# First attention's score core: maxima products ahead of the value products in each unit

## The chip, the cores and the metric

The kernel runs on one core of a Trainium2 chip. The metric is the device time of one execution in microseconds; lower is better. Three executions of the kernel before took 3728.84, 3730.03 and 3730.82 us, so its median is 3730.03 us.

## The reference

The whole program is four gated blocks of cross attention and feed-forward on a residual stream `x` of shape (4, 512, 512). The change is in the first attention only, which is this part of it:

```python
def _ln(t, w, b):
    m = jnp.mean(t, axis=-1, keepdims=True)
    v = jnp.var(t, axis=-1, keepdims=True)
    return (t - m) * jax.lax.rsqrt(v + EPS) * w + b
def _attn(q, k, v):
    s = jnp.einsum('bhqd,bhkd->bhqk', q, k) * SCALE
    p = jax.nn.softmax(s, axis=-1)
    return jnp.einsum('bhqk,bhkd->bhqd', p, v)
y_dca, y_main = y[:, -DCA:, :], y[:, :-DCA, :]          # DCA = 16 of the 512 context rows
q = _ln((x @ Wq + bq).reshape(b, s1, H, HD), qn_w, qn_b)  # H = 16 heads, HD = 32
ctx = _attn(qT, k, v)            # over the 496 main context rows
ctx_dca = _attn(qT, k_dca, v_dca)  # over the 16 others
ctx = ctx + DCA_WEIGHT * ctx_dca
return ctx @ Wo + bo
x = x + jnp.tanh(g_xattn[0]) * _L0_xattn_ref(_layernorm(x), ctx_1024, ...)
```

The later layers (a sign-weight feed-forward, a second attention, an int8 feed-forward, a state-space scan, two expert layers and a fourth attention with 32 heads) are not touched.

## The kernel before

Every layer is a run of blocks, and in a block each engine has its own program, in the order in which it is written; the programs meet at semaphores. The first attention has a weights block, a projection block, a core block and an output block. The change is in `attention_core_block` (L1640), in the branch for the first attention (`rope` false). The last attention calls the same function with `rope` true and takes the other branch.

**How the core is tiled.** There are 4 batches of 16 heads. A group is 2 heads of a batch (TG = 32 groups), and a unit is one of the 4 tiles of 128 context rows for the 2 heads of a group (TU = 128 units, UPG = 4 to a group). What a unit n needs of TensorE:

- `scores_t(n)` (L1841): two products of 128x512 into `ac_S`, the transposed scores. ScalarE takes their exponential into `ac_PT` (L1941).
- `values(n)` (L1857): the value products of the exponentials into `ac_o`, in float32. In the last unit of a group four more records follow, into `ac_t` (L1863), for the 16 other context rows.
- The softmax needs each query's maximum, and needs it before the scores. So separate maxima products (`scores(m)`, L1812) are made well ahead: 256 in all, 8 to a group (4 query tiles x 2 heads), the first 18 before any unit and then 2 to a unit through `more(n)` (L1879) until none is left, which is in the units 0 to 118. VectorE reduces each with two instructions (L1960 over 496 columns, L1962 over 16) into `ac_nmax`, and signals `max_done` (printed as maxima_81).
- Once the 8 maxima of a group are there, VectorE scales them into `ac_mx` (L1973), TensorE transposes them (`maxima_rows(g)`, L1829, in the first unit of a group, from `at_rows`), ScalarE copies the transposed rows to `ac_mrow` (L1932, signal `rows_ev`), and SyncE's queue sends them into a row of `QT` by four small DMAs (L1729). The scores of that later group then come out with the maximum subtracted.
- When a group is done, ScalarE copies `ac_o` and `ac_t` into `ac_oT` (L1923, L1925), TensorE transposes those in the next group's second and third unit (`group_transposes`, L1876), and VectorE divides by the sums and adds (L1984 to L1991, signal `a_done`). After each batch, the result is stored by a DMA of 1 MB (L1734), behind the row DMAs on the same queue, and VectorE's first division of the next batch waits for that.

**What sets the order.** TensorE's order is that of the loop below. ScalarE's is written too: in the first unit of a group it does the exponential, then the two copies L1923 and L1925 of the group before, which wait for the last value product; in the second unit the exponential, and behind it the copy of the rows, L1932.

**The ring.** `psM` has two slots. The maxima products and the transposed rows share them in turn, in the order in which the list `use` names them. A user may write only when the user two places before it has been read. The order in `use` is: two maxima, then, in a group's first unit, the rows.

```python
                for n in range(TU):
                    if n + 1 < TU:
                        scores_t(n + 1)
                    if n:
                        values(n - 1)
                    more(n)
                    if n in at_rows:
                        maxima_rows(at_rows[n])
```

Of the kernel before, what the change touches and what calls it, by code (L numbers as in the profile page):

```python
# [1639 lines left out]
def attention_core_block(nc, env, w, rope):  # L1640
# [20 lines left out]
    with ExitStack() as ctx:  # L1661
# [32 lines left out]
        def of_unit(n):  # L1694
            g, u = divmod(n, UPG)
            return g, u // NP, u % NP
# [19 lines left out]
        def chunk(g, i):  # L1716
            h = g % NG * GH + i
            return (h // 2, 64 * (h % 2), 64) if rope else (h, 0, P)
# [78 lines left out]
        def _(pe):  # L1797
# [6 lines left out]
            def scores(m):  # L1804
                g, j, i = of_maximum(m)
                b = g // NG
                if m % (NG * NMG) == 0 and b:
                    pe.wait_ge(kq_in[b % 2], 32 * ((b + 1) // 2 if b % 2 else b // 2))
                slot, previous = ring["max", m]
                reader_of(previous)  # L1810
                c, base, n = chunk(g, i)
                nc.tensor.matmul(psM[:, slot, :], QT[b % 2][base:base + n, j, c, :], KT[b % 2][base:base + n, :, c, :],  # L1812
                                 start=True, stop=True).then_inc(s_done, 1)

            def maxima_rows(g):
                pe.wait_ge(m_ready, g + 1)
                if rope:
                    if g >= 3:
                        pe.wait_ge(a_done, g - 2)
                    if g:  # L1820
                        pe.wait_ge(rows_ev, g)
                    bank = pd[:]
                else:
                    slot, previous = ring["rows", g]
                    reader_of(previous)
                    bank = psM[:, slot, :]
                out = bank.bitcast(F16)
                for j in range(TPB):
                    last = nc.tensor.transpose(out[0:NR, j * P:(j + 1) * P], mx[:, g % 2, j, :], env.id16[:])  # L1829
                last.then_inc(rows_T, 1)  # L1830

            def scores_t(n):
                g, kt, p = of_unit(n)
                b = g // NG
                if n % UPG == 0:
                    pe.wait_ge(row_in[g % 2], 16 * NR * (g // 2 + 1))
                if n >= 2:
                    pe.wait_ge(exp_done, n - 1)
                for i in range(2):
                    c, base, k = chunk(g, 2 * p + i)  # L1840
                    last = nc.tensor.matmul(psS[:, 2 * (n % 2) + i, :], KT[b % 2][base:base + k, kt, c, :],  # L1841
                                            QT[b % 2][base:base + k, :, c, :], start=True, stop=True)
                last.then_inc(sT_done, 1)

            def values(n):

                g, kt, _ = of_unit(n)
                b = g // NG
                if n + 1 - NP == b * UB:
                    pe.wait_ge(v_ready, b + 1)  # L1850
                if kt == 0 and g:
                    pe.wait_ge(o_ev, g)
                pe.wait_ge(exp_done, n + 1)
                for m in range(n + 1 - NP, n + 1):
                    for i in range(2):
                        r = 2 * of_unit(m)[2] + i
                        last = nc.tensor.matmul(po[r * VC:(r + 1) * VC, :], V[b % 2][:, kt, g % NG * GH + r, :],  # L1857
                                                PT[:, m % PTB, i, :], start=(kt == 0), stop=(kt == TPB - 1))
                if not rope and kt == TPB - 1:
                    if g:  # L1860
                        pe.wait_ge(a_done, g * NOUT)
                    for i in range(2):
                        last = nc.tensor.matmul(pd[i * VC:(i + 1) * VC, :], Vd[b % 2][:, g % NG * GH + i, :],  # L1863
                                                PT[:, n % PTB, i, :], start=True, stop=True)
                last.then_inc(pv_done, NP)

            def group_transposes(g, i):
                pe.wait_ge(o_ev if rope else oT_done, g + 1)
                if rope:
                    if g:  # L1870
                        pe.wait_ge(a_done, g)
                    pe.wait_ge(rows_ev, min(TG, g + 3))
                elif i:
                    pe.wait_ge(a_done, g * NOUT + i)
                for j in range(TPB):
                    last = nc.tensor.transpose(psT[:, j, :], oT[:, i, j * P:(j + 1) * P], env.id32[:])  # L1876
                last.then_inc(ot_T, 1)

            def more(n):  # L1879
                for m in range(AHEAD + 2 * n, min(TM, AHEAD + 2 * n + 2)):  # L1880
                    scores(m)
# [5 lines left out]
            if rope:  # L1887
                scores_t(1)
                for n in range(0, TU, 2):
                    if n + 2 < TU:  # L1890
                        scores_t(n + 2)
                    more(n)
                    values(n + 1)
                    more(n + 1)
                    if n + 3 < TU:
                        scores_t(n + 3)
                    for k in (n, n + 1):
                        if k in at_rows:
                            maxima_rows(at_rows[k])
                    if n % UPG == 2 and n > UPG:  # L1900
                        group_transposes(n // UPG - 1, 0)
            else:
                for n in range(TU):
                    if n + 1 < TU:
                        scores_t(n + 1)
                    if n:
                        values(n - 1)
                    more(n)
                    if n in at_rows:
                        maxima_rows(at_rows[n])  # L1910
                    if n >= UPG and n % UPG in (1, 2):
                        group_transposes(n // UPG - 1, n % UPG - 1)
                values(TU - 1)
# [964 lines left out]
```

## Time and profile before

| | |
|---|---|
| median of 3 executions | 3730.03 us (3728.84 to 3730.82) |
| profiled execution, its own time | 3727.34 us |
| its span | 3725.6 us |
| TensorE busy | 2626.4 us, 70% |
| VectorE busy | 2344.9 us, 63% |
| ScalarE busy | 1584.9 us, 43% |
| GpSimd busy | 997.7 us, 27% |

The core block of the first attention runs from 229 us to 622 us of this span, some 10% of it. The busy shares above are means over stages that have different limits, so they tell little of this block; it has to be read by its own stretches, and for a change of order by the timeline of one group, instruction by instruction. In a timeline row the time is the start, the next number the time from the first start to the last end, and in brackets is how long the engine had sat idle and what ended that. PEld is TensorE's loading of weights, which runs beside its products.

### The profile page before, as it was taken

The numbers are of one execution on the slowest core, as the hardware profiler recorded it, in microseconds if no ns is written. First come the engines' busy times: TensorE is split into PE (matmuls) and PEld (weight loads), VectorE is DVE, ScalarE is ACT, GpSimd is POOL, SyncE is SP. The second block draws the span as 40 slices with busy tenths as digits, with TensorE's granted clock in tenths as the row PEclk, the third lists the DMA queues.
The fourth block names the chain that finished last, engine by engine and source line by source line (L and its number), as shares of the span: only waits on it lengthen the run. The fifth ranks groups of instructions, "written<-read, shape, count | busy, mean of one in ns | idle before, by whom it ended". The sixth has DMA issues, their size and how long they took to land. (4 is left out here: it accounts for less than half of the span.)

```text
span 3725.6 us, 45742 instructions
## 1 busy us (share of the span) xinstructions
PE 2626.4 (70%) x13916; PEld 1206.9 (32%) x13916; DVE 2344.9 (63%) x4155; ACT 1584.9 (43%) x2191; POOL 997.7 (27%) x874
## 2 busy tenths in 40 slices
PE   3978888699665365275576559981978897748991
PEld 1532223344322122021121247760522222324660
DVE  6655664555735634598898766655668886455663
ACT  3544443144221034344444235551646766122870
POOL 5760000000000211376676322215640000001434
PEclk9979999799776587598898779995979999869995
DMA  3541101010000000000000157753531100112994
GB/s 128 204 153 71 57 12 57 15 46 34 0 3 9 19 0 0 0 1 0 0 0 0 46 182 239 237 173 113 219 140 69 46 12 24 65 49 79 321 304 153
DMA packets 148635, 305.98 MB, mean 82 GB/s; under 512 B 18323, under 2 KB 65439, under 8 KB 146038
## 3 DMA queue, kind: packets, MB, share of 16 engines
q1 hardware_dynamic: 125542, 223.49, 17.0%
q0 software_dynamic: 22928, 80.49, 6.8%
q8 instruction: 79, 1.29, 0.1%
q14 instruction: 86, 0.70, 0.1%
HBM read 210.34 MB, written 93.32 MB: 82 GB/s over the span
## 5 line engine op out<-in xcount | busy, mean ns | idle before, releaser
L1960 DVE TENSOR_REDUCE ac_nmax<-ac_M 128x1 f32<-128x512 f32 (+1 forms) x768 | 495.5, 680 | 197.8 <-PE ac_M L1812 196.0
L1941 ACT ACTIVATE ac_PT<-ac_S 128x1024 f32<-128x1024 f32 x384 | 380.5, 1018 | 220.4 <-PE ac_S L1841 220.4
L2680 PE MATMUL sc_y<-sc_hc,ident 128*128 128x512 f32 x512 | 294.0, 658 | 141.0 <-POOL sc_hc L2656 140.5
L2656 POOL TENSOR_TENSOR sc_hc<-sc_h,sc_cs 128x512 f32<-128x512 f32 x256 | 324.3, 1268 | 174.5 <-DVE sc_h L2758 170.6
L2758 DVE TENSOR_TENSOR_SCAN sc_h<-sc_dA,sc_dB 128x512 f32<-128x512 f32 x256 | 309.9, 1212 | 9.7 <-ACT sc_dA L2718 9.7
L1857 PE MATMUL ac_o<-ac_PT,ac_V 128*32 128x512 f32 (+1 forms) x1536 | 281.4, 621 | 7.4 <-ACT ac_PT L1941 7.0
L2718 ACT ACTIVATE sc_dA<-sc_dl,sc_A 128x512 f32<-128x512 f32 x256 | 176.4, 690 | 177.3 <-DVE sc_h L2758 177.3
L2680 PEld LDWEIGHTS sc_y<-sc_hc,ident 128*128 128x128 f32 x512 | 79.5, 193 | 333.6 <-POOL sc_hc L2656 330.5
L2750 DVE TENSOR_TENSOR sc_dB<-ss_du,sc_b 128x512 f32<-128x512 f32 x256 | 168.4, 659 | 15.8 <-PE sc_b L2670 15.8
L955 DVE SCALAR_TENSOR_TENSOR mo_up16l<-mo_up,mo_up16h 128x1408 f16<-128x1408 f32 (+1 forms) x80 | 117.1, 1465 | 72.8 <-ACT mo_up16h L899 72.1
L802 POOL DMA_INDIRECT mo_g<-normalised,mo_cur x112 | 145.8, 1302 | 61.3 <-POOL mo_cur L798 44.2
L2332 POOL TENSOR_TENSOR f_o<-f_o,f_bias 128x512 f16<-128x512 f32 x16 | 20.7, 1291 | 523.4 <-DVE f_o L2381 523.4
L1812 PE MATMUL ac_M<-KT,QT 64*128 64x512 f16 (+1 forms) x384 | 135.6, 425 | 32.7 <-DVE ac_nmax L1960 19.5
L855 PE MATMUL mo_pu<-mo_y16h,mo_up16h 128*128 128x256 f16 (+1 forms) x832 | 127.1, 276 | 27.5 <-DVE mo_up16l L955 12.6
L224 PE MATMUL ln_yt<-ident,ln_y 128*128 128x128 f32 x256 | 68.7, 433 | 103.1 <-DVE ln_y L200 103.1
L593 PE MATMUL ex_po<-ex_dn,ex_midh 128*128 128x512 f16 x384 | 137.6, 383 | 5.3 <-DVE ex_acc L657 5.3
L647 DVE SCALAR_TENSOR_TENSOR ex_midl<-ex_mid,ex_midh 128x512 f16<-128x512 f32 x80 | 55.2, 692 | 127.9 <-ACT ex_midh L540 127.9
L1812 PE MATMUL ac_M<-ac_KT,ac_QT 64*128 64x512 f16 (+1 forms) x384 | 120.4, 389 | 20.9 <-DVE ac_nmax L1960 18.5
L962 DVE SCALAR_TENSOR_TENSOR mo_dn16l<-mo_dn,mo_dn16h 128x1024 f16<-128x1024 f32 x80 | 83.0, 1062 | 71.2 <-ACT mo_dn16h L906 68.5
L1376 PE MATMUL ap_t<-ident,ap_y 128*128 128x128 f32 x128 | 20.4, 284 | 151.5 <-DVE ap_y L1562 151.5
L855 PE MATMUL mo_pu<-mo_y16l,mo_up16h 128*128 128x256 f16 (+1 forms) x832 | 125.8, 274 | 0.0
L855 PE MATMUL mo_pu<-mo_y16h,mo_up16l 128*128 128x256 f16 (+1 forms) x832 | 125.3, 273 | 0.0
(480 smaller groups left out, 5879.8 us busy)
## 6 DMA issues: line engine op xcount, KB each, us to landing
slot_results<-mo_o SPq DMA_DIRECT2D x56, 512.0 KB, 3.9
mo_up<-in_w_gate SPq DMA_DIRECT2D x24, 704.0 KB, 5.4
mo_up<-in_w_up SPq DMA_DIRECT2D x24, 704.0 KB, 7.1
keys_t<-ap_kto SPq DMA_DIRECT2D x32, 512.0 KB, 2.6
queries_t<-ap_qto SPq DMA_DIRECT2D x32, 512.0 KB, 2.7
mo_up<-in_exp_up SPq DMA_DIRECT2D x32, 512.0 KB
mo_dn<-in_exp_down SPq DMA_DIRECT2D x32, 512.0 KB
mo_dn<-in_w_down SPq DMA_DIRECT2D x24, 512.0 KB
```

The lines of the kernel that those rows point to most:

```text
L593: last = nc.tensor.matmul(po[j][:], (mid_h, mid_l)[a][0:n, tb % 2, c, j * P:(j + 1) * P], dn16[w][h][0:n, c, :], start=(i == 0), stop=(i = ...
L802: pool.indirect_dma_start(g[:, w, h, :], None, rows, bass.IndirectOffsetOnAxis(cur[:, w, h:h + 1], 0)).then_inc(g_in[w], 16)
L855: last = nc.tensor.matmul(pu[q][0:n, j, :], up16[h][:, w, j, k, c * P:c * P + n], y16[a][:, w, k, :], start=(i == 0), stop=(i == len(passe ...
L1812: nc.tensor.matmul(psM[:, slot, :], QT[b % 2][base:base + n, j, c, :], KT[b % 2][base:base + n, :, c, :], start=True, stop=True).then_inc( ...
L1857: last = nc.tensor.matmul(po[r * VC:(r + 1) * VC, :], V[b % 2][:, kt, g % NG * GH + r, :], PT[:, m % PTB, i, :], start=(kt == 0), stop=(kt ...
L1941: nc.scalar.activation(PT[:, n % PTB, :, :], psS[:, 2 * (n % 2):2 * (n % 2) + 2, :], ACT.Exp, scale=SCALE / (SQK * SQK)).then_inc(exp_done, 1)
L1960: last = v.tensor_reduce(out[:, :, 0], sc[:, 0:MAIN], AX.X, ALU.max)
L2656: nc.gpsimd.tensor_tensor(hc[:, m % RC, :], h[:, m % RH, :], cs[:, n % 2, :], ALU.mult).then_inc(hc_done, 1)
L2680: nc.tensor.matmul(py[:, c, :], env.id32[:], hc[:, m % RC, :], start=(n == 0), stop=(n == NS - 1)).then_inc(y_mm, 1)
L2718: nc.scalar.activation(dA[:, m % RA, :], dl[:, c, :], ACT.Exp, scale=A[:, c, n:n + 1]).then_inc(dA_done, 1)
L2750: nc.vector.tensor_tensor(dB[:, m % RB, :], at(du, b * KD + c), pb[:], ALU.mult).then_inc(dB_done, 1)
L2758: nc.vector.tensor_tensor_scan(h[:, m % RH, :], dA[:, m % RA, :], dB[:, m % RB, :], 0.0, ALU.mult, ALU.add).then_inc(h_done, 1)
```

## The change

In each unit the call `more(n)` (two maxima products) now stands ahead of `values(n - 1)` and not behind it. The list `use`, which gives the slots, is unchanged, and so are all other engines' programs.

```diff
@@ -1903,9 +1903,9 @@
                 for n in range(TU):
                     if n + 1 < TU:
                         scores_t(n + 1)
+                    more(n)
                     if n:
                         values(n - 1)
-                    more(n)
                     if n in at_rows:
                         maxima_rows(at_rows[n])
```

First place, TensorE where one group ends and the next begins (`ac_t<-ac_PT,ac_Vd` are the last value products of a group, `ac_M<-ident,ac_mx` the transposed rows; maxima_81 is the count of reduced maxima, rows_ev_84 the count of rows that ScalarE has copied, group_ev_88 ScalarE's copy of `ac_o`). Before:

```order
L1863 MATMUL ac_t<-ac_PT,ac_Vd 64x512 [waits attn_norm_91]
L1863 MATMUL ac_t<-ac_PT,ac_Vd 64x512
L1812 MATMUL ac_M<-KT_1,QT_1 128x512 [waits maxima_81] x2
L1829 MATMUL ac_M<-ident,ac_mx 4x128 [waits maxima_81,max_rows_82]
L1829 MATMUL ac_M<-ident,ac_mx 4x128 x3
L1841 MATMUL ac_S<-QT_1,KT_1 128x512 [waits exp_86]
L1841 MATMUL ac_S<-QT_1,KT_1 128x512
L1857 MATMUL ac_o<-ac_PT,ac_V 64x512 [waits exp_86,group_ev_88]
L1857 MATMUL ac_o<-ac_PT,ac_V 64x512
L1812 MATMUL ac_M<-KT_1,QT_1 128x512 [waits maxima_81]
L1812 MATMUL ac_M<-KT_1,QT_1 128x512 [waits rows_ev_84]
L1876 MATMUL ac_t<-ident,ac_oT 128x128 [waits group_copied_89]
```

The same place now:

```order
L1812 MATMUL ac_M<-KT_1,QT_1 128x512 [waits maxima_81] x2
L1857 MATMUL ac_o<-ac_PT,ac_V 64x512 [waits exp_86]
L1857 MATMUL ac_o<-ac_PT,ac_V 64x512
L1863 MATMUL ac_t<-ac_PT,ac_Vd 64x512 [waits attn_norm_91]
L1863 MATMUL ac_t<-ac_PT,ac_Vd 64x512
L1829 MATMUL ac_M<-ident,ac_mx 4x128 [waits maxima_81,max_rows_82]
L1829 MATMUL ac_M<-ident,ac_mx 4x128 x3
L1841 MATMUL ac_S<-QT_1,KT_1 128x512 [waits exp_86]
L1841 MATMUL ac_S<-QT_1,KT_1 128x512
L1812 MATMUL ac_M<-KT_1,QT_1 128x512 [waits maxima_81]
L1812 MATMUL ac_M<-KT_1,QT_1 128x512 [waits rows_ev_84]
L1857 MATMUL ac_o<-ac_PT,ac_V 64x512 [waits exp_86,group_ev_88]
```

The maxima products of the group's first unit moved from behind the `ac_t` products to ahead of the whole value step, and the transposed rows now follow the value products directly. Those of the second unit, the second of which waits for ScalarE's copy of the rows, moved from behind the value products of that unit to ahead of them.

Second place, TensorE in the third and fourth unit of a group, from its second transpose of results on (attn_norm_91 is `a_done`, row_in0_77 the landing of the row DMAs). Before:

```order
L1876 MATMUL ac_t<-ident,ac_oT 128x128 [waits attn_norm_91,group_copied_89]
L1876 MATMUL ac_t<-ident,ac_oT 128x128 x3
L1841 MATMUL ac_S<-QT_1,KT_1 128x512 [waits exp_86,row_in0_77]
L1841 MATMUL ac_S<-QT_1,KT_1 128x512
L1857 MATMUL ac_o<-ac_PT,ac_V 64x512 [waits exp_86]
L1857 MATMUL ac_o<-ac_PT,ac_V 64x512
L1812 MATMUL ac_M<-KT_1,QT_1 128x512 [waits maxima_81] x2
L1841 MATMUL ac_S<-QT_1,KT_1 128x512 [waits exp_86]
```

And now:

```order
L1876 MATMUL ac_t<-ident,ac_oT 128x128 [waits attn_norm_91,group_copied_89]
L1876 MATMUL ac_t<-ident,ac_oT 128x128 x3
L1841 MATMUL ac_S<-QT_1,KT_1 128x512 [waits exp_86,row_in0_77]
L1841 MATMUL ac_S<-QT_1,KT_1 128x512
L1812 MATMUL ac_M<-KT_1,QT_1 128x512 [waits maxima_81] x2
L1857 MATMUL ac_o<-ac_PT,ac_V 64x512 [waits exp_86]
L1857 MATMUL ac_o<-ac_PT,ac_V 64x512
L1841 MATMUL ac_S<-QT_1,KT_1 128x512 [waits exp_86]
```

Here the pair of maxima moved ahead of the value products too. The orders of VectorE, ScalarE, GpSimd and SyncE are the same before and now.

## Rows read from the trace of the kernel before

**Rows 1.** Stretches; columns: us, busy us of PE, PEld, DVE, ACT, POOL (instructions), PEclk, DMA share, GB/s

```profile
273.89:338.90 65.01, 60.82 (x288) 20.34 (x288) 43.87 (x133) 32.20 (x43) 7.54 (x8) 1.00 0.09 33
440.00:450.00 10.00, 8.24 (x40) 2.70 (x36) 5.83 (x18) 3.07 (x4) 0.23 (x1) 1.00 0.45 179
460.00:468.00 8.00, 7.81 (x23) 2.38 (x24) 3.86 (x13) 1.02 (x1) 0.00 (x0) 0.60 0.00 0
```

**Rows 2.** Waits, 244 to 622 us: who waited for whom, us, times, longest

```profile
PE ac_M L1829 <- DVE ac_nmax L1962: 21.5, 30, 0.7
PE ac_t L1876 <- DVE ac_A L1986: 10.9, 3, 3.6
```

**Rows 3.** Timeline of PE, one full group, 500 to 512 us

```profile
500.50 0.60 PE L1812 MATMUL ac_M<-KT,QT 128*128 128x512 f16 x2
501.83 0.38 PE L1829 MATMUL ac_M<-ident,ac_mx 128*4 128x128 f16 x4 [0.72 <-DVE ac_nmax L1962]
502.14 0.61 PE L1841 MATMUL ac_S<-QT,KT 128*128 128x512 f16 x2
502.68 1.08 PE L1857 MATMUL ac_o<-ac_PT,ac_V 128*64 128x512 f32 x4
503.69 0.60 PE L1812 MATMUL ac_M<-KT,QT 128*128 128x512 f16 x2
504.13 0.60 PE L1876 MATMUL ac_t<-ident,ac_oT 128*128 128x128 f32 x4
506.55 0.60 PE L1876 MATMUL ac_t<-ident,ac_oT 128*128 128x128 f32 x4
506.99 0.59 PE L1841 MATMUL ac_S<-QT,KT 128*128 128x512 f16 x2
509.49 1.08 PE L1857 MATMUL ac_o<-ac_PT,ac_V 128*64 128x512 f32 x4
510.40 1.03 PE L1863 MATMUL ac_t<-ac_PT,ac_Vd 128*64 128x512 f32 x4
511.36 0.60 PE L1812 MATMUL ac_M<-ac_KT,ac_QT 128*128 128x512 f16 x2
```

**Rows 4.** Timeline of ACT, the same group

```profile
500.61 0.60 ACT L1923 ACTIVATE ac_oT<-ac_o 128x512 f32<-128x512 f32 x1 [2.83 <-PE ac_t L1863]
501.11 0.59 ACT L1925 ACTIVATE ac_oT<-ac_t 128x512 f32<-128x512 f32 x1
501.58 1.03 ACT L1941 ACTIVATE ac_PT<-ac_S 128x1024 f32<-128x1024 f32 x1
502.49 0.57 ACT L1932 ACTIVATE ac_mrow<-ac_M 4x512 f16<-4x512 f16 x1
```

**Rows 5.** Timeline of DVE, the same group

```profile
500.93 0.68 DVE L1960 TENSOR_REDUCE ac_nmax<-ac_M 128x1 f32<-128x496 f32 x1 [1.34 <-PE ac_M L1812]
507.87 0.20 DVE L1984 RECIPROCAL ac_rec<-ac_t 128x8 f32<-128x8 f32 x1
508.95 0.67 DVE L1960 TENSOR_REDUCE ac_nmax<-ac_M 128x1 f32<-128x496 f32 x1
510.28 0.16 DVE L1962 TENSOR_REDUCE ac_nmax<-ac_M 128x1 f32<-128x16 f32 x1
```

**Rows 6.** Timeline, 238 us: PEld waiting for the copy of the rows

```profile
238.00 0.59 ACT L1932 ACTIVATE ac_mrow<-ac_M 4x512 f16<-4x512 f16 x1 [15.97 <-PE ac_M L1829]
...
238.63 0.10 PEld L1812 LDWEIGHTS ac_M<-KT,QT 128*128 128x128 f16 x1 [0.51 <-ACT ac_mrow L1932]
```

**Rows 7.** Timeline of PE where it sat idle longer

```profile
445.97 0.61 PE L1841 MATMUL ac_S<-QT,KT 128*128 128x512 f16 x2 [1.76 <-DMA QT<-ac_mrow]
460.19 1.08 PE L1876 MATMUL ac_t<-ident,ac_oT 128*128 128x128 f32 x4 [3.62 <-DVE ac_A L1986]
467.93 0.61 PE L1812 MATMUL ac_M<-KT,QT 128*128 128x512 f16 x2
609.27 0.61 PE L1841 MATMUL ac_S<-ac_QT,ac_KT 128*128 128x512 f16 x2 [1.53 <-DMA ac_QT<-ac_mrow]
```

## The prediction

> **What bounds the kernel now.** The change touches only the core block of the first attention, so I read that block alone, in four steps. First the table of stretches: in steady state TensorE is busy 60.82 of 65.01 us at a granted clock of 1.00, while VectorE has 43.87 and ScalarE 32.20 [rows 1]. TensorE is the bound there, with a gap of about 7%. Then the list of waits: 30 times TensorE waited for VectorE ahead of the transposed rows (L1829), 21.5 us in all and never more than 0.7; and 3 times, up to 3.6 us, for a division that itself waits for the store at the end of a batch [rows 2]. Then the timeline of one group, which tells what the gap is. In the first unit of a group the two maxima products start at 500.50; each takes half of 0.44 (503.69 to 504.13 is a pair). The transposed rows take the ring slot of the first of them, so they wait until that one is reduced, and start at 501.83: 501.83 - 500.50 - 0.44 = 0.89 us in which TensorE issues nothing [rows 3]. VectorE starts the reduction only 0.43 after the product starts [rows 5]. From 500.50 to the same place at 511.36 a group takes 10.86 us [rows 3]; of the 30 distances between transposed rows in the timeline 23 have this length.
>
> The last view is ScalarE's timeline beside it, since the ring has a second edge. The second maxima product behind the transposed rows takes their slot, and must wait until ScalarE has copied them (the order prints it as the wait for rows_ev). In a group's first unit ScalarE copies `ac_o` at 500.61 and `ac_t` at 501.11, when the last value product is done; then comes an exponential at 501.58, and only then the copy of the rows, from 502.49 to 503.06 [rows 4]. Before the change the product that needs it is due at 503.69 + 0.22 = 503.91 [rows 3], so that edge costs nothing, with 0.8 us to spare.
>
> **The change, term by term, for one full group.** I call 0 the moment at which TensorE has issued the last value product of a group (500.50 in the trace of before). Nothing is added or removed; 119 pairs of maxima products move ahead of 118 value steps (unit 0 has none), and on each side of a value product the neighbours change.
>
> *Removed:* the 0.89 us. The maxima of the first unit now come ahead of the value products and the `ac_t` products, 1.9 us (509.49 to 511.36 [rows 3]) earlier. Their first reduction is over before the rows are due, by over half a microsecond. The rows can start at 0.
>
> *Added:* the wait for ScalarE. It can't be moved, because its two copies are released by the last value product as before, and ScalarE's order is the same; so the copy of the rows still ends at 503.06 - 500.50 = 2.56. Where the trace shows TensorE waiting for this copy, the weights load starts at 238.63 for a copy that ends at 238.59, so 0.04 later [rows 6]: the second maximum goes at 2.60. Without the wait it would go at 0.97, that is, rows 0.31 (501.83 to 502.14), scores 0.44, first maximum 0.22. The new wait is 1.63 us. What is queued behind the waiting product: the value products, the transposes and the scores of the next units, in short all that TensorE has. No other engine relieves it. The value products of the second unit now start at 2.60 + 0.22 + 0.10 = 2.92, where the 0.10 is what the scores before a value step take beyond a pair's 0.44 (502.14 to 502.68 is 0.54). Before it was 502.68 - 500.50 = 2.18 [rows 3]. **So this part of the group gets 0.74 us longer**, the removed gap counted in.
>
> *Behind that,* from these value products to the next 0: before 8.68 us (502.68 to 511.36), now the same instructions, three pairs of maxima among them as before, so 8.68 again, if nothing new waits.
>
> *A second wait, small:* VectorE in the third and fourth unit. The second transpose of results is issued at 2.92 + 3.87 - 0.44 = 6.35 (before it, 502.68 to 506.55, stood one pair more), and ends at 6.95. VectorE's division and addition follow at about 7.00 and take 1.08 (507.87 to 508.95), then two maxima 1.49 (508.95 to 510.44) [rows 5]: 9.57. The second maximum of the next first unit needs that slot at 6.35 + 0.44 + 0.44 + 0.54 + 1.01 + 0.44 + 0.22 = 9.44 (transpose, scores, pair, values, scores, one maximum). It waits some 0.2 us. Before, this reduction had the value products in between.
>
> *A possible saving:* a value step takes 1.01 when float16 products follow (502.68 to 503.69) and 0.91 when float32 ones do (509.49 to 510.40) [rows 3]. Now the transposes of results, which are float32, follow a value step directly in two units of a group. The trace has no such pair of neighbours, so this is worth 0 to 0.2 us a group; I take half.
>
> Sum for a full group: + 0.74 + 0.2 - 0.1 = **+ 0.84 us**, with bounds of + 0.5 (no second wait, all of the saving) and + 1.1 (no saving, second wait of 0.35). Over 23 full groups that is 19.3 us.
>
> *The seven other distances* hold a stall by a DMA or are the first or the last. Three of them hold the wait for the store of a batch [rows 2]. The store is queued behind the row DMAs, which start with the copy of the rows, at the same 2.56; so TensorE is released there at the same moment as before, and both the removed gap and the new wait vanish in that stall. What remains is one pair of maxima more between release and next 0, 0.44, or twice that at the lower clock, and part of the second wait. The groups where scores wait for a late row DMA work in the same way. I take + 0.6 for six of these, 3.6, and 0 for the first (there ScalarE has no results to copy, so the gap goes and little comes). In all **+ 23 us**.
>
> The clock. After the batch stall of 3.62 us the products run slower until 467.93 [rows 7]; over 460 to 468 the granted clock is 0.60 [rows 1], that is, mostly the 1.2 GHz level. But after waits of 1.76 and 1.53 us at 445.97 and 609.27 products take the same time as before (0.61 for a pair) [rows 7], and over 440 to 450 it is 1.00 [rows 1]. The new wait, 1.63 less the tail of the product before it, is a little under these. So I price the clock at nothing.
>
> Against that stands a rule of the Trainium skill (TensorE: Matmul & The Clock Gate, A second HAM failure mode): a kernel whose TensorE idles briefly but often between groups of products can swing between the two clock levels. By it the sum would be that of the clock rival below. The trace so far disagrees, with 30 gaps of 0.7 us at 1.00.
>
> **Numbers.** The profiled execution took 3727.3 us, 2.7 below the median of 3730.0, which is within what executions differ. 3727.3 + 23 = 3750 for a profiled one, 3730 + 23 = **3753 us** for the median. About 0.2%, or 7.5 us, is what a measurement of this kernel can tell from no change.
>
> **Rivals.**
> - *Faster: the copy of the rows is not late.* If something frees the slot within a microsecond, the 0.89 goes 30 times and little comes: - 27 us, 3703. It decides at a wait of 0.89: below it the change gains. For it: the exponential ahead of the copy has its scores early, and ScalarE sat idle 2.83 us before it [rows 4]. Against: the exponential is written behind both copies, which wait for the last value product, and the order of ScalarE is unchanged; the trace shows these four back to back. 5%.
> - *No change: the two about cancel.* If float16 to float32 switches save 0.1 us in most of 119 units rather than in 60, 8 to 10 us come back, and without the second wait (4 us) the sum is + 23 - 9 - 5 = + 9, 3739; a little more puts it below 7.5. For it: the 0.10 is seen at both sides of a value step. Against: in a unit without transposes the number of switches stays. 6%.
> - *Much slower: the clock.* If each new wait brought the lower level, as the batch stall does, then the stretch from the second transpose to the next 0 takes 467.93 - 460.19 = 7.74 in place of 511.36 - 506.55 = 4.81 [rows 3, 7], 2.9 us a group, 29 times: + 85, so 3730 + 23 + 85 = 3838. 4%.
> - My forecast has the other 85%: 23 x 0.5 plus little, + 12, at one end, 23 x 1.1 and 1 us for each other group, + 32, at the other.
>
> Faster by over 0.2%: 5%. Within: 6%. Slower by over 0.2%: 89%. Forecast's own span is 3742 to 3762; for 8 in 10, with the spread of runs and the cancelling case's upper part, 3738 to 3768.
>
> **What would show it.** In the profile after: the wait of L1829 for VectorE gone; a new wait of the second maximum (L1812) for `ac_mrow` L1932, some 30 times, 1.4 to 1.6 us each; a distance between transposed rows of 11.6 to 11.9 us in place of 10.86; a few tenths of waiting for `ac_nmax` once a group; a granted clock of 1.00 in the steady stretches; ScalarE's four rows in the same spacing. The block from first scores to last should be some 23 us longer, and every later block the same. If L1812 doesn't wait for L1932, the main step is wrong; if the distance is under 10.9, so is the sign; if the clock falls in steady groups, the size is.

## The result: 23 to 30 us slower, with a new wait behind the transposed rows

| | before | after |
|---|---|---|
| median, first comparison | 3729.78 us (4 runs) | 3759.70 us (4 runs, 3758.02 to 3761.70), ratio 1.0080, 95% interval 1.0063 to 1.0098 |
| median, the change once more | 3727.82 us (19 runs) | 3750.96 us (4 runs, 3750.04 to 3760.30), ratio 1.0067, 1.0047 to 1.0087 |
| span of the profiled execution | 3725.6 us | 3759.9 us, and 3748.2 us in the second |
| core block, from its first product to the first of the output block | 405.7 us | 432.4 us, and 429.1 us |

The change costs 30 us by the first comparison and 23 us by the second. In the core block it is 26.8 us in the first profile and 23.4 in the second; the rest, in the first profile only, lies in blocks that the change does not touch (see the last section). Of the 26.8 and 23.4 us, 2.1 and 0.7 come before the first unit's transposed rows, where TensorE's order is still that of before and the first scores wait for their row DMA (3.39 us before, 5.46 and 4.14 after).

The profile after. First the table of stretches over six full groups (71.23 us, against 65.01 in [rows 1]):

```profile
273.75:344.98 71.23, 62.36 (x290) 20.68 (x288) 44.49 (x132) 32.40 (x42) 5.85 (x7) 1.00 0.08 28
```

The clock is 1.00 as before. The stretch is 6.2 us longer and TensorE's busy time 1.5 us more, so 4.7 us of the loss are plain idle time. The rest is the tails of products that now stand alone (0.38 and 0.39 where a pair shows 0.60) and slower transposes, both seen in the timeline below. The list of waits of TensorE from 262 us to the end of the block says which:

```profile
PE ac_M L1812 <- ACT ac_mrow L1932: 42.9, 29, 1.5
PE ac_t L1876 <- DVE ac_A L1986: 10.9, 4, 3.4
PE ac_S L1841 <- DMA ac_QT<-ac_mrow: 5.3, 2, 3.8
```

The waits of L1829 for VectorE, 21.5 us in [rows 2], are gone from here on. In their place stand 42.9 us, 29 times, in which the second maximum waits for ScalarE's copy of the rows. The waits for the store at batch ends are nearly what they were (3.36 us each, against 3.62 [rows 7]; the fourth in the list, 0.85 us, stands at the end of the block and stood there before too, behind the window of [rows 2]). The timeline of TensorE in one full group, to be laid beside [rows 3]:

```profile
504.65 0.39 PE L1829 MATMUL ac_M<-ident,ac_mx 128*4 128x128 f16 x4
504.97 0.60 PE L1841 MATMUL ac_S<-QT,KT 128*128 128x512 f16 x2
505.41 0.38 PE L1812 MATMUL ac_M<-KT,QT 128*128 128x512 f16 x1
507.27 0.39 PE L1812 MATMUL ac_M<-KT,QT 128*128 128x512 f16 x1 [1.48 <-ACT ac_mrow L1932]
507.59 1.08 PE L1857 MATMUL ac_o<-ac_PT,ac_V 128*64 128x512 f32 x4
508.60 0.66 PE L1876 MATMUL ac_t<-ident,ac_oT 128*128 128x128 f32 x4
509.09 0.59 PE L1841 MATMUL ac_S<-QT,KT 128*128 128x512 f16 x2
...
513.96 0.77 PE L1812 MATMUL ac_M<-KT,QT 128*128 128x512 f16 x2
514.66 1.08 PE L1857 MATMUL ac_o<-ac_PT,ac_V 128*64 128x512 f32 x4
515.57 1.03 PE L1863 MATMUL ac_t<-ac_PT,ac_Vd 128*64 128x512 f32 x4
516.52 0.39 PE L1829 MATMUL ac_M<-ident,ac_mx 128*4 128x128 f16 x4
```

And ScalarE beside it, to be laid beside [rows 4]:

```profile
504.77 0.60 ACT L1923 ACTIVATE ac_oT<-ac_o 128x512 f32<-128x512 f32 x1 [3.43 <-PE ac_t L1863]
505.26 0.59 ACT L1925 ACTIVATE ac_oT<-ac_t 128x512 f32<-128x512 f32 x1
505.74 1.03 ACT L1941 ACTIVATE ac_PT<-ac_S 128x1024 f32<-128x1024 f32 x1
506.65 0.57 ACT L1932 ACTIVATE ac_mrow<-ac_M 4x512 f16<-4x512 f16 x1
```

The moment called 0 in the prediction is 504.65. The rows go there without a gap. ScalarE's four instructions have the spacing of before to 0.02 us, the copy of the rows ends at 507.22, that is at 2.57, and the second maximum goes at 2.62. Had it been free it would have gone at 505.63, 0.22 behind the first: a wait of 1.64 us in TensorE's issue (the profile lists 1.48, since the product before it was still running). The distance from one group's transposed rows to the next is 11.87 us, against 10.86, in 23 of 30 cases.

Three small terms are visible too, one wait and two slower transposes. The pair at 513.96 takes 0.70 and not 0.53 until the value products follow, so 0.17 of waiting for VectorE. And each of the two transposes of results, now directly behind a value step, takes 0.49 (508.60 to 509.09) where it took 0.44 [rows 3].

So a full group can be written as a ledger. Without any wait and with the neighbours of before it is 10.86 - 0.89 = 9.97 us. Add 1.64 + 0.17 + 2 x 0.05: 11.88, against 11.87 measured.

### The profile page after: what moved, and what is told of

It reads as the page before. It is cut to its first block and busy times, and to the rows that moved or that the text cites. A ratio compares the mean times of both kernels' runs of the same rounds, so it can differ in the third digit from the quotient of the medians.

```text
span 3759.9 us, 45742 instructions
## 1 busy us (share of the span) xinstructions
PE 2641.8 (70%) x13916; PEld 1211.9 (32%) x13916; DVE 2349.0 (62%) x4155; ACT 1586.3 (42%) x2191; POOL 1000.4 (27%) x874
```

## The experiments

Two theories were set against each other. A: the loss is the ring's second edge, the wait for ScalarE's copy of the rows. B: it comes from the value products' new neighbours and from waits for VectorE, in all units alike. Each kernel's group length comes from the distances between the L1829 rows of its timeline, most of which agree to a few hundredths; the ratio is to the kernel before on the same chip. Each was compared with 19 to 23 runs of before.

### e1: the pair of the second unit stays behind

```diff
-                    more(n)
+                    if n % UPG in (0, 2, 3):
+                        more(n)
                     if n:
                         values(n - 1)
+                    if n % UPG not in (0, 2, 3):
+                        more(n)
```

> The change is kept in the first, third and fourth unit of a group; in the second unit the two maxima go behind the value products as before. Theory A (the loss is the wait of the second maximum in the second unit for ScalarE's copy of the rows, at 2.60 us behind the last value product of the group): that maximum is then due at 0.31 + 0.54 + 1.01 + 0.22 = 2.08, the wait falls from 1.48 to about 0.5 us and lies behind the value products; I expect a group of about 10.9 us and 3730 to 3740 us. Theory B (the loss comes from the new neighbours of the value products and from waits for VectorE in all units alike): only a quarter of the 30 us goes, 3750 us or more.

Measured: 3734.6 us median (10 runs), ratio 1.0021, 1.0010 to 1.0033; most groups 10.86 us. TensorE from one group to the next:

```profile
498.60 0.61 PE L1841 MATMUL ac_S<-QT,KT 128*128 128x512 f16 x2
...
503.42 0.39 PE L1829 MATMUL ac_M<-ident,ac_mx 128*4 128x128 f16 x4
503.73 0.60 PE L1841 MATMUL ac_S<-QT,KT 128*128 128x512 f16 x2
504.27 1.08 PE L1857 MATMUL ac_o<-ac_PT,ac_V 128*64 128x512 f32 x4
505.28 0.39 PE L1812 MATMUL ac_M<-KT,QT 128*128 128x512 f16 x1
506.03 0.39 PE L1812 MATMUL ac_M<-KT,QT 128*128 128x512 f16 x1 [0.36 <-ACT ac_mrow L1935]
```

The second maximum waits 506.03 - 505.50 = 0.53, not 1.64, though three of four pairs are still ahead: theory A. But the gap is not won back. The scores at 498.60 wait for the row DMAs, whose landing nobody had waited for in a full group of before; the weights row says so:

```profile
498.60 0.12 PEld L1841 LDWEIGHTS ac_S<-QT,KT 128*128 128x128 f16 x2 [0.38 <-DMA QT<-ac_mrow]
```

Their due time was 498.29 (0.49 behind the transposes at 497.80), so they wait 0.31. Ledger: 9.97 + 0.53 + 0.31 + 0.05 = 10.86. That a group is as long as before is a coincidence: two new waits and a slower transpose add up to the gap that was removed.

### e2: ScalarE copies the rows ahead of the exponential

```diff
-                before = n - (3 if rope else 1)
+                before = n - (3 if rope else 0)
                 if before in at_rows:
                     group_rows(at_rows[before])
```

> TensorE's order is that of the change; ScalarE copies the rows directly behind its two copies of results and ahead of the exponential of the second unit. Theory A: the copy ends 0.91 us earlier (502.49 less 501.58 in the trace of before), the wait of the second maximum falls from 1.48 to about 0.6 us, a group from 11.87 to 11.0, and the time by 29 x 0.9 = 26 us to about 3734 us. Theory B (neighbours and VectorE): no change, 3760 us.

Measured: 3728.67 us (10 runs), ratio 1.0000, 0.9990 to 1.0010; groups 10.97 us. TensorE's order is exactly that of the change:

```profile
500.40 0.38 PE L1812 MATMUL ac_M<-KT,QT 128*128 128x512 f16 x1
501.35 0.39 PE L1812 MATMUL ac_M<-KT,QT 128*128 128x512 f16 x1 [0.57 <-ACT ac_mrow L1932]
```

The wait in the issue falls from 1.64 to 501.35 - 500.62 = 0.73, by the 0.91 that the exponential took, and the group by 0.90. The ledger closes here too: 9.97 + 0.73 + 0.17 + 0.10 = 10.97. The whole loss of time went with ScalarE's order; this is what theory A asks, and theory B is out as the main cause.

### e3: only the first unit's pair ahead

The set `(0, 2, 3)` of e1 is `(0,)` here.

> Only in the first unit of a group the two maxima go ahead of the value products. This takes the 0.89 us gap ahead of the transposed rows away and leaves the second unit as it was. If that gap is a loss of its own, 23 to 27 us are gained: 3705 us. If, as a count of VectorE's steps says, the pair of the fourth unit (still behind its value products) and this pair now lie only a pair and the scores apart (0.44 + 0.44 us, against 2 x 0.67 us of reductions), TensorE waits for VectorE there instead: some 0.9 us, and the rows copy is waited for by 0.5 us more: then no gain but a loss, 3740 to 3750 us.

Measured: 3755.89 us (4 runs), ratio 1.0072, 1.0055 to 1.0089; groups 11.76 us. The sign is that of the second guess, the size is above it.

```profile
503.56 0.60 PE L1841 MATMUL ac_S<-QT,KT 128*128 128x512 f16 x2 [0.20 <-DMA QT<-ac_mrow]
...
505.55 0.59 PE L1841 MATMUL ac_S<-QT,KT 128*128 128x512 f16 x2
506.35 0.39 PE L1812 MATMUL ac_M<-KT,QT 128*128 128x512 f16 x1 [0.20 <-DVE ac_nmax L1965]
507.09 0.39 PE L1812 MATMUL ac_M<-KT,QT 128*128 128x512 f16 x1 [0.35 <-DVE ac_nmax L1965]
...
511.89 0.39 PE L1812 MATMUL ac_M<-KT,QT 128*128 128x512 f16 x1 [0.36 <-ACT ac_mrow L1935]
```

Against their due times (505.99, 0.22 behind the first, 0.22 again, and 0.44 behind the transposes) these wait 0.36 + 0.52 for VectorE, 0.53 for ScalarE and 0.36 for the row DMA, 1.77 in all, for the 0.89 taken away: 9.97 + 1.77 = 11.74. I had left out the row DMA. Removing the only gap of a group, and nothing else, makes it 0.9 us longer.

### e6: only the second unit's pair ahead

The set is `(1,)`.

> Only in the second unit of a group do the two maxima go ahead of the value products; the gap ahead of the transposed rows stays. The second maximum is due at 1.33 + 0.31 + 0.44 + 0.22 = 2.30 us behind the last value product and waits for the copy of the rows till 2.60: 0.3 us, 29 times, 9 us: 3738 us. So the edge costs 1.6 us only where the gap ahead of it is gone; if it cost the full 1.5 us here too, it would be 3770 us.

Measured: 3735.47 us (10 runs), ratio 1.0016, 1.0007 to 1.0026; groups 11.22 us, + 0.36, where 0.3 was counted. The pair at 505.56 takes 0.84 until the value products, in place of 0.53: a wait of 0.31, and one transpose of results is 0.05 longer. So where the rows go 1.33 us later, as before the change, the same edge costs 0.3 and not 1.64:

```profile
504.80 0.38 PE L1829 MATMUL ac_M<-ident,ac_mx 128*4 128x128 f16 x4 [0.72 <-DVE ac_nmax L1965]
505.12 0.60 PE L1841 MATMUL ac_S<-QT,KT 128*128 128x512 f16 x2
505.56 0.92 PE L1812 MATMUL ac_M<-KT,QT 128*128 128x512 f16 x2
506.40 1.08 PE L1857 MATMUL ac_o<-ac_PT,ac_V 128*64 128x512 f32 x4
```

### e7: only the third and fourth unit's pairs ahead

The set is `(2, 3)`.

> Only in the third and fourth unit of a group do the maxima go ahead of the value products. The gap of 0.89 us stays, the rows are not waited for. What can cost here: the third unit's pair now follows the second unit's (still behind its value products) after the transposes and scores only, 0.88 us, against 1.34 us of two reductions: a wait for VectorE of about 0.4 us; and transposes directly behind value products, 0.05 us. A group of 11.3 us, 3740 us. If waits for VectorE don't matter, 3730 us.

Measured: 3734.21 us (10 runs), ratio 1.0018, 1.0008 to 1.0028; groups 11.28 us. The third unit's second maximum waits 0.37 for VectorE (498.81 against 498.44), and one transpose is 0.05 longer: 9.97 + 0.89 + 0.37 + 0.05 = 11.28. So theory B's causes exist. In the change itself they are worth 0.17 + 0.10 = 0.27 us of a group, against 1.64.

```profile
497.79 0.59 PE L1841 MATMUL ac_S<-QT,KT 128*128 128x512 f16 x2
498.22 0.38 PE L1812 MATMUL ac_M<-KT,QT 128*128 128x512 f16 x1
498.81 0.39 PE L1812 MATMUL ac_M<-KT,QT 128*128 128x512 f16 x1 [0.21 <-DVE ac_nmax L1965]
```

The parts don't add: over the kernel before, the first unit's pair alone is + 0.90 us, the second's + 0.36, the third's and fourth's + 0.42, together + 1.68; all of them at once are + 1.01.

### e4 and e8: the rows behind the next scores

e4 has the order of before, except that the rows go one step later:

```diff
                     if n + 1 < TU:
                         scores_t(n + 1)
+                    if n - 1 in at_rows:
+                        maxima_rows(at_rows[n - 1])
                     if n:
                         values(n - 1)
                     more(n)
-                    if n in at_rows:
-                        maxima_rows(at_rows[n])
```

> The order of the kernel before, but the transposed rows go behind the scores of the next unit and not ahead of them, so that these 0.44 us of scores fill the gap in which the rows wait for the first reduction. ScalarE's copy of the rows comes late in any case (2.56 us), so nothing waits for them sooner. Theory A (the gap of 0.89 is idle time of the bounding engine): it falls to about 0.35 to 0.45, some 0.5 us in 30 groups, 15 us: 3715 us. Rival: the gap only moves to another wait, 3730 us.

Measured: 3718.66 us (6 runs), ratio 0.9974, 0.9961 to 0.9986; groups 10.42 us. The scores fill the first half of the gap: 495.94 - 495.05 - 0.44 = 0.45 is left.

```profile
495.05 0.59 PE L1841 MATMUL ac_S<-QT,KT 128*128 128x512 f16 x2
495.94 0.38 PE L1829 MATMUL ac_M<-ident,ac_mx 128*4 128x128 f16 x4 [0.29 <-DVE ac_nmax L1962]
496.25 1.08 PE L1857 MATMUL ac_o<-ac_PT,ac_V 128*64 128x512 f32 x4
```

e8 is e4 with the copy of the rows ahead of ScalarE's exponential, as in e2.

> The kernel e4 (the order of before, the rows behind the next scores), and ScalarE copies the rows ahead of the second unit's exponential. In that order nothing waits for the copy, so it should bring 0 to 2 us against e4: 3717 to 3719 us. If ScalarE's order matters by itself and not by the wait behind the rows, it moves by more.

Measured: 3718.19 us (10 runs), ratio 0.9973, 0.9964 to 0.9983; groups 10.32 us in place of 10.42. In that order ScalarE's order is worth what was expected, next to nothing, where in the change it was worth 0.90 us a group.

### e5, e10 and e11: the copy of the rows first

e5 has TensorE's order of the change, and ScalarE copies the rows ahead of both copies of results:

```diff
+                before = n - (3 if rope else 0)
+                if not rope and before in at_rows:
+                    group_rows(at_rows[before])
                 if u == 0 and g:
                     group_out(g - 1)
-                before = n - (3 if rope else 1)
-                if before in at_rows:
+                if rope and before in at_rows:
                     group_rows(at_rows[before])
```

> TensorE's order is that of the change; ScalarE copies the transposed rows ahead of its two copies of results. The rows are issued at the last value product, so their copy ends at about 0.45 + 0.57 = 1.0 us in place of 2.56, and the second maximum (due at 0.97) hardly waits. What is late next: the copy of results ends at 1.6 us, and the value products of the second unit wait for it till about 1.65, against 1.3 without any wait. Theory A: a group of 10.5 to 10.7 us, 7 to 9 us under the kernel before, 3721 us. Theory B: no change against the changed kernel, 3760 us.

Measured: 3712.44 us (4 runs), ratio 0.9948, 0.9929 to 0.9968; groups 10.47 us. It is faster than the kernel before, and a group is 0.5 us above the 9.97 without any wait. TensorE and ScalarE where a group begins:

```profile
483.96 0.39 PE L1829 MATMUL ac_M<-ident,ac_mx 128*4 128x128 f16 x4
484.28 0.60 PE L1841 MATMUL ac_S<-QT,KT 128*128 128x512 f16 x2
484.38 0.59 ACT L1932 ACTIVATE ac_mrow<-ac_M 4x512 f16<-4x512 f16 x1 [3.74 <-PE ac_M L1829]
484.72 0.69 PE L1812 MATMUL ac_M<-KT,QT 128*128 128x512 f16 x2
484.88 0.57 ACT L1923 ACTIVATE ac_oT<-ac_o 128x512 f32<-128x512 f32 x1
485.50 1.08 PE L1857 MATMUL ac_o<-ac_PT,ac_V 128*64 128x512 f32 x4
```

The copy of the rows ends at 1.01 us, as counted, and the value products wait 0.25 (due 0.53 behind 484.72) for the copy of `ac_o`, which ends at 485.45. Ledger: 9.97 + 0.25 + 0.17 + 0.10 = 10.49.

e10 takes the same order of ScalarE with TensorE's order of before.

> TensorE's order is that of the kernel before, and ScalarE's is that of e5 (rows copied ahead of the results). It tells whether e5's gain is ScalarE's order alone. Count: the rows are issued at 1.33 us behind the last value product, their copy holds ScalarE till about 2.3, so the copy of ac_o ends at about 2.85 and the value products of the second unit, due at 2.18, wait for it for 0.7 us: a group of 11.5 us, 20 us slower than before, 3747 us. If e5's gain came from ScalarE's order alone, this one would be near 3712 us.

Measured: 3735.85 us (10 runs), ratio 1.0022, 1.0012 to 1.0033; groups 11.54 us, as counted, since the value products now wait for the copy of `ac_o`; the time is not the 3747 us expected:

```profile
496.17 0.61 PE L1841 MATMUL ac_S<-QT,KT 128*128 128x512 f16 x2
497.39 1.08 PE L1857 MATMUL ac_o<-ac_PT,ac_V 128*64 128x512 f32 x4 [0.61 <-ACT ac_oT L1923]
```

23 groups of + 0.68 would be 16 us; the time went up by only 8. In its profile the seven other distances are 3.9 us shorter in sum: two with a stall are 13.71 and 14.44 us, where the kernel before has 17.15 and 17.56, and three others are longer, by up to 1.2. At the batch ends TensorE is released 9.60 us behind the last value product there, against 9.83 in the kernel before, since the row DMAs and the store behind them start earlier; that is 0.7 us in three stalls, so most of the 3.9 has no shown cause. So neither order gains by itself: TensorE's alone costs 23 to 30 us, ScalarE's alone 8, both together gain.

e11 is e5 once more.

> e5 once more, in more rounds, to tell its distance from the kernel before: 14 to 17 us faster, 3711 to 3715 us, if its first result holds; nearer to 8 us, 3720 us, if the single executions of the first run were low ones.

Measured: 3710.00 us (6 runs), ratio 0.9954, 0.9939 to 0.9970. Both runs of this kernel are 15 to 18 us faster than the kernel before, and it is the best of all that were run. The full groups account for only 23 x 0.39 = 9 us of that. The other seven distances are 13.9 and 8.3 us shorter than before in the two profiles; the next section tells what they hold.

### e9: the change once more

> The changed kernel once more, as it is. The first pair of profiles showed 26.8 us more in the core block and 7.5 us more in blocks that the change does not touch. If those 7.5 us belong to the change, the blocks behind the core take as long as in its first profile, 3100 us from the output block's first product to the end; if they are scatter of single executions, they lie between 3090 and 3100 us here.

Measured: 3750.96 us (4 runs). Groups are 11.87 us again, with the same 1.48 ahead of the second maximum. Behind the core block it takes 3748.2 - 656.6 = 3091.6 us, as the kernel before does (3725.6 - 634.2 = 3091.4); in the first profile of the change it was 3100.2.

## Why the prediction was right, step by step

- *The bound, and the gap of 0.89 us.* Right: the gap is gone in the profile after. That it was worth something only if nothing took its place was the point of the prediction, and e3 shows it without the rest of the change.
- *The added wait.* Right. ScalarE's copy was forecast to end at 2.56 and the maximum to go at 2.60; they did at 2.57 and 2.62. The value products of the second unit were forecast at 2.92 and came at 2.94. e2 and e5 show that it is this wait that carries the loss: with the copy 0.91 earlier a group is 0.90 shorter, and with the copy first it is 1.40 shorter.
- *The second wait, for VectorE:* forecast 0.2, measured 0.17.
- *The possible saving:* this term failed. I took - 0.1 for float32 transposes directly behind float32 value products. The value step in front of them still takes 1.01, and each transpose takes 0.05 more, so it is + 0.10. That is the difference between + 0.84 forecast for a full group and + 1.01 measured, or 4 us over 23 groups.
- *The seven other distances:* forecast + 3.6 us, and here the mechanism was right in one part and the size came by luck. From the first transposed rows inside a unit to the last there were 354.34 us before, and 378.77 and 377.26 in the two profiles after. Less 23 x 1.01, the seven make + 1.2 and - 0.3. But one by one they moved by - 2.0 to + 1.7, where + 0.6 was forecast for each of six. Right was that the stalls at batch ends take up both the gap and the wait: TensorE is released there 9.83 us behind the last value product in every profile of the kernel before and of the change. It also follows the copy of the rows, as the prediction had it: with that copy 0.91 earlier (e2) the release comes at 8.93, with it 1.55 earlier (e5, e11) at 8.28, and in e10, where it ends at 2.34, so 0.22 earlier, at 9.60. What was not foreseen is how much the clock differs behind the release (next point). And the last distance, where no maxima are left ahead of its rows, had no gap to remove; it pays the full new wait and 0.10 for the two transposes, + 1.73.
- *The sum:* + 23 was forecast. From the first unit's rows to the last it is + 24.4 and + 22.9, in the whole block + 26.8 and + 23.4. That it comes so near owes something to two misses that partly cancel: the saving that did not come, 4 us over 23 groups, and the seven distances, 2.4 and 3.9 us below their forecast.
- *The clock:* right at nothing, 1.00 over the full groups with 29 waits of 1.48 us. The rule of the Trainium skill (TensorE: Matmul & The Clock Gate, A second HAM failure mode), that frequent short idle times between groups of products can make TensorE swing between its clock levels, did not show at this length and spacing. A full group is 11.87 us in both profiles. Behind the stalls at batch ends the clock is not the same from one to the next, and no term of the prediction had that: before, the stretches from the release to the next transposed rows took 9.01, 9.06 and 7.75 us (the gap of 0.89 included) at a granted clock of 0.66, 0.66 and 0.78; after, in the first profile, 7.83, 6.90 and 8.15 us at 0.65, 0.75 and 0.63. In e5, whose waits there are 3.20 us, they took 5.85, 5.85 and 6.57 us at 1.00, 1.00 and 0.79, and in e11, the same kernel, 6.91, 8.01 and 6.99 us at 0.75, 0.64 and 0.76. So part of what e5 and e11 gain over the full groups is clock, part is the earlier release; what decides the clock of a single stall stays open.
- *The rivals.* The faster one needed the slot free by 0.89 us; it decides where it was said to. e5 is that rival made true: with the copy done at 1.01 the value products of the second unit wait 0.25 in its place, and the group gets shorter than before. No change and the fallen clock did not occur.

## What to carry to other kernels

A ring of buffers has an edge for each of its users, and moving one user closer to another shortens the time that each edge had. Write down, for every wait of the moved instruction, when its releaser is done and what sets that: here the releaser stood behind an exponential on an engine that was less than half busy. Filling a gap in the bounding engine pays only if the work that is pulled forward finds all its inputs and slots ready; it can take a change of order on a second engine, which by itself is worth next to nothing (e8) or costs time (e10), to make it so. And where a group's work fits into the gap without moving any other wait, as the scores do in e4, one engine's order is enough.

## What the runs showed beyond that

Comparing one profile with another overstates the precision. Behind the core block the program is the same in all these kernels, yet the time from the output block's first product to the end lay between 3090.5 us (e4) and 3100.2 us (the first profile of the change). About half of the first profile's excess over the kernel before (4.0 of 8.8 us) is in the stretch of the scan's preparation, where the first row is of before and the second of the change:

```profile
1284.00:1570.00 286.00, 128.44 (x451) 49.47 (x449) 124.27 (x143) 106.96 (x106) 59.52 (x31) 0.70 0.02 6
```

```profile
1311.00:1601.00 290.00, 133.01 (x451) 50.54 (x449) 124.35 (x143) 106.56 (x105) 59.58 (x31) 0.68 0.02 6
```

Nearly the same instructions, and TensorE busy for 4.6 us more at a granted clock of 0.68 in place of 0.70. The second profile of the change has 290.2 us there as well and still comes to 3091.6 for the whole, so no part of this can be charged to the change, or to anything else, from these runs. It stays open what sets it. Between the two profiles of the change, 3759.9 and 3748.2 us, it makes 8.6 of the 11.7 us, with the same 11.87 us a group in both. That the first comparison gave 30 us and the second 23 for this reason is likely but not shown, since only one execution of each comparison has a trace.
